# A gather-and-sum layer on one core: groups of 11 edge tiles made into batches of 22, each engine one batch behind its source, W1 applied after the last edge

## Chip, cores and metric

One core of a Trainium2 chip. The metric is the device time of one execution in microseconds (us); less is better.

## What is computed

A graph layer over 6,250 nodes of 96 features and 106,250 edges sorted by destination. Cut to what matters:

```python
h = jnp.maximum(_layernorm(x, axis=-1), 0.0)
ea = edge_attr @ W_edge.T + b_edge
msg = jax.nn.relu(h[src] + ea)
aggr = jax.ops.segment_sum(msg, dst, num_segments=N_NODES)
z = (1.0 + eps) * h + aggr
out = x + jax.nn.relu(z @ W1.T + b1) @ W2.T + b2
```

All data is float32. The edges make 830 tiles of 128 and a tail of 10.

## The kernel before

**Tiles and groups.** The 830 tiles are worked on in 77 groups (`group_sizes`, L43): 7 of ten tiles, 68 of eleven, 2 of six. In each group all but at most one tile get their rows `h[src]` by an indirect DMA that POOL issues (`gather`, L286: one instruction per tile). The eleventh tile is gathered by TensorE: a one-hot matrix (VectorE, `make_onehot`, L608, 125 x 6400 in bf16) times `h` split into three bf16 parts (`split_table`, L590), in 50 matmuls of 288 columns (`gather_by_matmul`, L390), which also add that tile's edge term (L396); VectorE then sums the three parts (L636).

**A group, by engine.** TensorE makes the edge terms of the ten tiles, two groups ahead (`edge_features`, L381, two banks per group, two groups of banks). VectorE adds the gathered rows, five tiles at once (L641). ScalarE applies relu (L362). TensorE multiplies each tile of messages by a 0/1 matrix `select` (VectorE, L546), which sums them by destination into a window of 128 nodes (L427). VectorE copies the window (L567), moves the offsets (L568), and makes the next `select`; TensorE multiplies the copy by W1 (L431); VectorE adds the product to `acc` (L578). A group has one window. `acc` so holds z @ W1 from the start.

**Order.** Each engine's program is written out by hand. TensorE per group g: sums of g, W1 of g (it waits for the copy), one-hot gather of g+1, edge terms of g+2 (L449 to L465). VectorE per group g: parts of g's one-hot gather (waits for TensorE), additions of g, one-hot of g+2, then the window of g (L619 to L662). POOL may be five groups ahead (`GATHER_RING`): it waits for VectorE's additions of g-5 (L306). SyncE loads edges three groups ahead, and the source numbers for the one-hots (`load_pe_src`, L249) in chunks of 17 tiles.

**Front.** Layernorm of all nodes in five chunks (VectorE statistics L510, ScalarE L333), the table `h` stored to DRAM (L247); POOL gathers 30 tiles of raw `x` meanwhile, which are normalised afterwards (L628 to L633, L355); table gathers wait for the store (L299). In groups 2 to 14 the term (1 + eps) * h @ W1 is made in 13 steps (transposes L440, copy L340, matmul L447, addition L586).

**End.** For ten blocks of 625 nodes: relu with b1 (L375), matmuls with W2 (L472), addition of x (L669), store (L272).

Of the kernel before, what the change touches and what calls it, by code (L numbers as in the profile page):

```python
# [7 lines left out]
ALU = mybir.AluOpType  # L8
# [7 lines left out]
GROUP_TILES = 10  # L16
# [4 lines left out]
RAW_GROUPS = 3  # L21
LAST_TILES = 6
PE_FROM = 7
PE_AHEAD = 2
SRC_CHUNK = 17
SPLITS = 3
GATHER_RING = 5
EDGE_RING = 3
NODE_PARTS = 125
NODE_RUN = 5  # L30
LN_COLS = 10
BASE_COLS = 4
BASE_FROM = 2
BOUND_ROWS = 80

# [7 lines left out]
def group_sizes(tiles):  # L43

    rest = tiles - 2 * LAST_TILES - PE_FROM * GROUP_TILES
    paired = rest // (GROUP_TILES + 1)
    assert paired * (GROUP_TILES + 1) == rest
    return [(GROUP_TILES, 0)] * PE_FROM + [(GROUP_TILES, 1)] * paired + [(LAST_TILES, 0)] * 2


def gnn_layer(nc, x, edge_t, src_tiles, pe_src, dst_tiles, dst_rows, w_edge_t, b_edge,
# [4 lines left out]
    pairs = group_sizes(TILES)  # L56
    sizes = [by_pool for by_pool, _ in pairs]
    tiles_of = [by_pool + by_pe for by_pool, by_pe in pairs]
    pe_index = [sum(by_pe for _, by_pe in pairs[:g]) if pairs[g][1] else None for g in range(len(pairs))]
    PE_TILES = sum(by_pe for _, by_pe in pairs)  # L60
    GROUPS = len(sizes)
    LAST = GROUPS - 1
    MOST = max(tiles_of)
    GE = MOST * EDGE_TILE
# [4 lines left out]
    HALF = HALF_TILES * D  # L69
    first_tile = [sum(tiles_of[:g]) for g in range(GROUPS)]  # L70
    halves = [[(t, min(t + HALF_TILES, n)) for t in range(0, n, HALF_TILES)] for n in sizes]
    adds_to = [sum(len(h) for h in halves[:g]) for g in range(GROUPS + 1)]
    gathers_to = [[sum(halves[k][i][1] - halves[k][i][0] for k in range(g % GATHER_RING, g + 1, GATHER_RING)
                       if i < len(halves[k])) for i in range(len(halves[g]))] for g in range(GROUPS)]
# [3 lines left out]
    SRC_CHUNKS = PE_TILES // SRC_CHUNK  # L78
    HS = SPLITS * D
    SRCS = SRC_CHUNK * EDGE_TILE  # L80
    assert sum(tiles_of) == TILES and PE_TILES % SRC_CHUNK == 0 and PE_FROM >= LN_CHUNKS + 1 and N == BLOCKS * BLOCK and COLS % LN_COLS == 0 and GROUPS <= BOUND_ROWS
    assert 0 < TAIL and HALF <= BANK and D + WINDOW // 4 == WINDOW and (RUN - 1) * D + WINDOW <= BANK
# [5 lines left out]
    with ExitStack() as ctx:  # L88
# [136 lines left out]
        def edges_of(g):  # L225
            return edge_t[:, first_tile[g] * EDGE_TILE:(first_tile[g] + tiles_of[g]) * EDGE_TILE]
# [49 lines left out]
        def _(pool):  # L276
# [18 lines left out]
            for g in range(RAW_GROUPS):  # L295
                for t in range(GROUP_TILES):
                    gather(x, g, t)
# [420 lines left out]
```

## Time and profile before

| | |
|---|---|
| median of 3 runs | 1468.35 us (1465.48 to 1468.41) |
| the profiled execution: time | 1468.4 us |
| its span, first to last instruction | 1466.3 us |
| mean granted TensorE clock | 0.858 of 2.4 GHz |
| POOL gathers of a tile | 762, and one of the tail |
| groups with a one-hot gather | 68 |

The time of the profiled execution is 2.1 us over its span. PE is TensorE's matmuls, PEld its weight loads, DVE VectorE, ACT ScalarE, POOL GpSimd, SPq SyncE's queue. A busy time counts neither register work nor waits, so an engine that is 56% busy can still set the time in a part of each period. L12 is line 12 of the kernel before. A timeline line has: start, duration, engine, line, operation, output<-input, count of merged instructions and, in brackets, the engine's idle time before it and what ended it.

### The profile page before, as it was taken

What the parts mean: (1) busy time and instruction counts of PE and PEld (TensorE: products, weight loads), DVE (VectorE), ACT (ScalarE), POOL (GpSimd) and SP (SyncE); (2) the same over time, 40 slices, a digit from 0 to 9 for tenths busy, and PEclk for the clock granted to TensorE, in tenths of its full rate; (3) what the DMA queues carried; (4) which work ended last, traced back from release to release, by engine and by line L of the source; (5) the groups of instructions that cost most, each with busy time, mean ns of one, the idle gap of its engine ahead of it and who ended that gap; (6) DMA issues with size and microseconds to landing.
All of it is one profiled execution on the core that took longest, in us unless ns stands there. A gap on an engine that the chain in (4) does not pass through costs nothing.

```text
span 1466.3 us, 18251 instructions
## 1 busy us (share of the span) xinstructions
PE 1033.7 (70%) x7058; PEld 842.1 (57%) x7058; DVE 825.7 (56%) x806; ACT 144.9 (10%) x270; POOL 731.9 (50%) x771
## 2 busy tenths in 40 slices
PE   2023477777677777777777777777777777777777
PEld 2023365555566666665666666665666666666566
DVE  4424556545555566656655656666566555656643
ACT  4302101001000001000000000000000000000002
POOL 7345654445455555555555555555555555555200
PEclk9966667988899989989889899999888899989985
DMA  8411131221422232222222322222222222222102
GB/s 217 103 40 39 44 94 47 51 54 42 113 64 60 57 86 70 61 59 60 58 60 60 87 58 60 70 59 60 58 60 56 60 60 57 65 64 60 37 9 66
DMA packets 39302, 94.84 MB, mean 65 GB/s; under 512 B 15049, under 2 KB 17549, under 8 KB 38719
## 3 DMA queue, kind: packets, MB, share of 16 engines
q1 hardware_dynamic: 14031, 55.61, 13.8%
q0 software_dynamic: 24416, 37.51, 12.6%
q8 instruction: 58, 0.95, 0.3%
q10 hardware_dynamic: 772, 0.57, 0.2%
q14 instruction: 25, 0.20, 0.0%
HBM read 88.82 MB, written 4.80 MB: 64 GB/s over the span
## 4 chain that ended last, share of the span: by engine, by line
PE 48%; DVE 26%; issue 19%; another core or an unknown queue 3%; ACT 3%; DVEq 2%
PE pe_ps L394 36%; DVE onehot L612 15%; DVE msg L641 6%; PE sums_ps L427 4%; PE sums_ps L431 3%; PE edge_ps L385 2%; PE edge_ps L472 2%; ACT msg L362 1%; DVE agg_sb L567 1%; PE pe_ps L396 1%; ACT gathered L355 1%; PE base_ps L447 1%; DVEq L622 1%; DVE stats L510 1%
## 5 line engine op out<-in xcount | busy, mean ns | idle before, releaser
L289 POOL DMA_INDIRECT gathered<-h_table,src_all x732 | 701.5, 958 | 616.8 <-DVE msg L641 415.0
L394 PE MATMUL pe_ps<-hs_or_hidden,onehot 125*128 125x288 bf16 x3400 | 538.6, 327 | 6.1 <-issue 4.3
L394 PEld LDWEIGHTS pe_ps<-hs_or_hidden,onehot 125*128 125x128 bf16 x3400 | 376.1, 112 | 156.4 <-issue 20.3
L612 DVE TENSOR_TENSOR onehot<-iota_bank,x_all 125x6400 bf16<-125x6400 f32 x68 | 463.4, 6815 | 0.1
L427 PE MATMUL sums_ps<-select,msg 128*96 128x128 f32 x1660 | 228.3, 301 | 136.5 <-ACT msg L362 123.5
L427 PEld LDWEIGHTS sums_ps<-select,msg 128*96 128x96 f32 x1660 | 213.2, 184 | 156.3 <-issue 156.3
L636 DVE TENSOR_REDUCE msg<-pe_ps 128x96 f32<-128x288 f32 x68 | 31.1, 458 | 396.0 <-PE pe_ps L396 393.1
L431 PE MATMUL sums_ps<-agg_sb,w 96*96 96x128 f32 x154 | 43.7, 374 | 233.8 <-DVE agg_sb L567 197.6
L385 PE MATMUL edge_ps<-w_edge,edge_in 97*128 97x96 f32 x1524 | 191.1, 283 | 22.4 <-DMA edge_in<-edge_t_dram 22.4
L362 ACT ACTIVATE msg<-msg 128x480 f32<-128x480 f32 (+2 forms) x154 | 94.5, 634 | 1106.0 <-DVE msg L641 1106.0
L385 PEld LDWEIGHTS edge_ps<-w_edge,edge_in 97*128 97x128 f32 x1524 | 184.6, 199 | 22.6 <-issue 22.6
L431 PEld LDWEIGHTS sums_ps<-agg_sb,w 96*96 96x96 f32 x154 | 23.0, 196 | 251.2 <-DVE agg_sb L567 211.3
L546 DVE TENSOR_TENSOR select<-iota_bank,dst_rel 128x1408 f32<-128x1408 f32 (+2 forms) x78 | 124.7, 1599 | 17.0 <-DVE dst_rel L568 12.8
L641 DVE TENSOR_TENSOR msg<-edge_ps,gathered 128x480 f32<-128x480 f32 (+1 forms) x154 | 92.6, 643 | 13.2 <-ACT gathered L355 11.3
L586 DVE TENSOR_TENSOR acc<-acc,base_ps 96x500 f32<-96x500 f32 (+1 forms) x13 | 13.6, 1048 | 96.8 <-PE base_ps L447 92.1
L567 DVE COPY agg_sb<-sums_ps 96x128 f32<-96x128 f32 x77 | 21.4, 278 | 52.9 <-PE sums_ps L427 21.6
L289 POOL DMA_INDIRECT gathered<-x_dram,src_all x30 | 28.5, 952 | 9.9 <-issue 8.8
L396 PE MATMUL pe_ps<-w_edge,edge_in 97*128 97x96 f32 x136 | 24.4, 260 | 0.0
L578 DVE TENSOR_TENSOR acc<-acc,sums_ps 96x128 f32 x77 | 21.1, 274 | 4.4 <-remote 4.4
L472 PE MATMUL edge_ps<-w,hs_or_hidden 97*125 97x128 f32 x100 | 22.1, 424 | 1.7 <-ACT hs_or_hidden L375 1.7
L472 PEld LDWEIGHTS edge_ps<-w,hs_or_hidden 97*125 97x125 f32 x100 | 21.8, 311 | 2.0 <-ACT hs_or_hidden L375 2.0
L396 PEld LDWEIGHTS pe_ps<-w_edge,edge_in 97*128 97x128 f32 x136 | 21.4, 191 | 1.7
(65 smaller groups left out, 179.1 us busy)
## 6 DMA issues: line engine op xcount, KB each, us to landing
edge_in<-edge_t_dram SPq DMA_DIRECT2D x68, 528.0 KB
gathered<-h_table,src_all POOLq DMA_INDIRECT x732
x_all<-pe_src_dram SPq DMA_DIRECT2D x4, 952.0 KB
edge_in<-edge_t_dram SPq DMA_DIRECT2D x7, 480.0 KB
x_all<-x_dram SPq DMA_DIRECT2D x5, 420.0 KB
h_table<-h_all SPq DMA_DIRECT2D x5, 420.0 KB
h_all<-x_dram SPq DMA_DIRECT2D x1, 2100.0 KB
out_dram<-h_all SPq DMA_DIRECT2D x10, 210.0 KB
```

Of the source, the lines that this page charges most:

```text
L289: nc.gpsimd.indirect_dma_start(out=gathered[slot][:, t * D:(t + 1) * D], out_offset=None, in_=table, in_offset=bass.IndirectOffsetOnAxis(a ...
L362: nc.scalar.activation(half, half, ACT.Relu).then_inc(relu_done, 1)
L385: mm = pe.matmul(edge_ps[g % 2][t // HALF_TILES][:, at:at + D], edge_in[g % EDGE_RING][:, t * EDGE_TILE:(t + 1) * EDGE_TILE], w_edge[:], s ...
L394: pe.matmul(pe_ps[:, 0:HS], onehot[k % 2][:, j, :], hs[:, j, :], start=(j == 0), stop=False)
L396: pe.matmul(pe_ps[:, 0:D], edge_in[g % EDGE_RING][:, sizes[g] * EDGE_TILE:tiles_of[g] * EDGE_TILE], w_edge[:], start=False, stop=True).the ...
L427: mm = pe.matmul(agg_ps[0:D, :], data, select[0:rows, t, :], start=(t == 0), stop=(t == tiles - 1))
L431: pe.matmul(z_ps[0:D, :], w1[:], agg_sb[:], start=True, stop=True).then_inc(fold_done, 1)
L472: mm = pe.matmul(edge_ps[c % 2][c // 2 % 2][0:NP, i * D:i * D + WINDOW], hidden_nodes[:, c, i, :], w2[:], start=True, stop=True)
L546: nc.vector.tensor_tensor(select[:, 0:tiles, :], iota_ps.unsqueeze(1).broadcast_to((128, tiles, WINDOW)), dst_rel[:, bass.ds(at, tiles)].u ...
L567: nc.vector.tensor_copy(agg_sb[:], agg_ps[0:D, :]).then_inc(agg_copied, 1)
L612: nc.vector.tensor_tensor(onehot[k % 2][:], column_ps.unsqueeze(2).broadcast_to((NP, COLS, EDGE_TILE)), node_of[:, at:at + EDGE_TILE].unsq ...
L641: nc.vector.tensor_tensor(msg[g % 2][:, t0 * D:t1 * D], edge_ps[g % 2][i][:, 0:(t1 - t0) * D], gathered[slot][:, t0 * D:t1 * D], ALU.add). ...
```

## The change

The tiles are worked on in 39 batches of two sides: 3 batches of 2 x 10 tiles, 34 of 2 x 11 (ten by POOL, one by TensorE on each side), one of 12 and one of 10. POOL's gathers (762 and the tail) and TensorE's one-hot gathers (68) stay the same in number. `GATHER_RING` 5 groups becomes `SLOTS` 2 batches, in gathers and in edges. Both sides share one `select` instruction and one set of edge banks; each side has its own window, so there are 39 rounds of sums for 77.

W1 is taken out of the windows (L431 and the copy L567 go; VectorE adds the sums straight to `acc`, once per side) and is applied after the last edge, per block of 625 nodes, in two matmuls of 320 and 305 columns (`hidden_sums`). The base term (1 + eps) * h is written to `acc` before the first window, by 13 groups of transposes and 13 VectorE instructions; it needs no matmul with W1. Only 20 tiles are gathered raw, 8 at once and 12 after the layernorm's second half. The layernorm's small operations are done for 20 and 30 columns instead of five times ten.

TensorE per turn c: sums of c-1, edge terms of c+1, one-hot gathers of c+1. VectorE per turn c: additions of c, parts of c's one-hot gathers, window of c-1, the two one-hots of c+2. Core of the diff:

```diff
-GROUP_TILES = 10
+SIDE_TILES = 10
+SIDES = 2
-GATHER_RING = 5
-EDGE_RING = 3
+SLOTS = 2
-SRC_CHUNK = 17
+SRC_CHUNK = 14
+PLAIN_BATCHES = 3
+LAST_SIDES = (6, 5)
+Z_SPLIT = 320
...
             # POOL
+            for s, t in first[:FIRST_BURST]:
+                gather(x, 0, s, t)
+            pool.wait_ge(norm_ready, 2)
+            for s, t in first[FIRST_BURST:]:
+                gather(x, 0, s, t)
             pool.wait_ge(src_rest_in, 16)
             pool.wait_ge(table_stored, 16 * len(spread) * LN_CHUNKS)
...
-            for g in range(RAW_GROUPS, GROUPS):
-                if g >= GATHER_RING:
-                    pool.wait_ge(added, adds_to[g - GATHER_RING + 1])
-                for t in range(sizes[g]):
-                    gather(h_table, g, t)
+            for c in range(1, BATCHES):
+                for s, t0, t1 in halves[c]:
+                    if c >= SLOTS:
+                        pool.wait_ge(added, adds_to[c - SLOTS] + half_at[c - SLOTS][(s, t0)] + 1)
+                    for t in range(t0, t1):
+                        gather(h_table, c, s, t)
...
             # TensorE
+            def edge_features(c):
+                pe.wait_ge(edges_in[c % SLOTS], 16 * (c // SLOTS + 1))
+                for i, (s, t0, t1) in enumerate(halves[c]):
+                    if c >= 1:
+                        before = half_at[c - 1][(s, t0)]
+                        pe.wait_ge(added, adds_to[c - 1] + before + 1)
...
+            def gather_by_matmul(c):
+                for s in range(SIDES):
+                    k = pe_before[c] + s
+                    pe.wait_ge(onehot_made, k + 1)
+                    if k >= SIDES:
+                        pe.wait_ge(pe_rows_summed, k - SIDES + 1)
...
-                    pe.wait_ge(agg_copied, this_window)
-                    pe.matmul(z_ps[0:D, :], w1[:], agg_sb[:], start=True, stop=True).then_inc(fold_done, 1)
...
+            for c in range(BATCHES):
+                if c >= 1:
+                    sum_windows(c - 1)
+                if c + 1 < BATCHES:
+                    if c == 0:
+                        pe.wait_ge(ones_set, 2)
+                    edge_features(c + 1)
+                    if has_pe[c + 1]:
+                        if pe_before[c + 1] == 0:
+                            pe.wait_ge(hs_made, LN_CHUNKS)
+                            pe.wait_ge(tail_added, 1)
+                        gather_by_matmul(c + 1)
+            sum_windows(LAST)
+
+            def hidden_sums(c):
+                if c >= 2:
+                    pe.wait_ge(mlp_relu_done, len(z_parts) * (c - 1))
+                for i, (n0, n1) in enumerate(z_parts):
+                    pe.matmul(z_banks[c % 2][i][0:D, 0:n1 - n0], w1[:], acc[:, c * BLOCK + n0:c * BLOCK + n1],
+                              start=True, stop=True).then_inc(z_done, 1)
...
             # VectorE
-                    nc.vector.tensor_copy(agg_sb[:], agg_ps[0:D, :]).then_inc(agg_copied, 1)
+                    dve.wait_ge(acc_summed, this_window)
+                    add_sums(0, firsts[0], done).then_inc(side_summed, 1)
...
                     make_select(dve.snap(over, min_val=at, max_val=at + step), widest)
-                    dve.wait_ge(fold_done, this_window)
-                    dve.wait_ge(acc_summed, this_window)
-                    nc.vector.tensor_tensor(acc[:, bass.ds(base, WINDOW)], acc[:, bass.ds(base, WINDOW)],
-                                            z_ps[0:D, :], ALU.add).then_inc(acc_summed, 1)
+                    dve.wait_ge(side_summed, this_window)
+                    add_sums(1, firsts[1], done).then_inc(acc_summed, 1)
...
+            for c in range(BATCHES):
+                slot = c % SLOTS
+                dve.wait_ge(edge_done, c + 1)
+                for s, t0, t1 in halves[c]:
+                    i = t0 // HALF_TILES
+                    dve.wait_ge(gather_in[slot][s][i], 16 * gathers_to[c][(s, t0)])
...
+                if has_pe[c]:
+                    for s in range(SIDES):
+                        at = s * side[c] + by_pool[c]
+                        dve.wait_ge(pe_gathered, pe_before[c] + s + 1)
...
+                if c >= 1:
+                    sum_windows(c - 1)
+                if c == 0:
+                    split_table([0, 1, 2])
+                if c == 1:
+                    split_table([3, 4])
+                if c + 2 < BATCHES and has_pe[c + 2]:
+                    if c == 2:
+                        dve.wait_ge(table_stored, 16 * len(spread) * LN_CHUNKS)
+                    make_onehots(c + 2)
```

## Rows read from the trace of the kernel before

**Rows 1.** The page: busy time by engine, and the chain that ended last, by engine.

```profile
PE 1033.7 (70%) x7058; PEld 842.1 (57%) x7058; DVE 825.7 (56%) x806; ACT 144.9 (10%) x270; POOL 731.9 (50%) x771
...
PE 48%; DVE 26%; issue 19%; another core or an unknown queue 3%; ACT 3%; DVEq 2%
```

**Rows 2.** The timeline of one group of eleven tiles, all engines but POOL.

```profile
705.95 2.40 PE L385 MATMUL edge_ps<-w_edge,edge_in 97*128 97x96 f32 x20
706.15 0.46 DVE L636 TENSOR_REDUCE msg<-pe_ps 128x96 f32<-128x288 f32 x1 [6.66 <-PE pe_ps L396]
...
706.53 1.21 DVE L641 TENSOR_TENSOR msg<-edge_ps,gathered 128x480 f32<-128x480 f32 x2
...
707.66 6.82 DVE L612 TENSOR_TENSOR onehot<-iota_bank,x_all 125x6400 bf16<-125x6400 f32 x1
...
708.77 2.62 PE L427 MATMUL sums_ps<-select,msg 128*96 128x128 f32 x22 [0.43 <-ACT msg L362]
...
714.39 0.28 DVE L567 COPY agg_sb<-sums_ps 96x128 f32<-96x128 f32 x1
...
714.72 0.46 PE L431 MATMUL sums_ps<-agg_sb,w 96*96 96x128 f32 x2 [3.33 <-DVE agg_sb L567]
...
714.96 1.62 DVE L546 TENSOR_TENSOR select<-iota_bank,dst_rel 128x1408 f32<-128x1408 f32 x1 [0.22 <-DVE dst_rel L568]
715.01 8.26 PE L394 MATMUL pe_ps<-hs_or_hidden,onehot 125*128 125x288 bf16 x50
...
723.51 0.46 DVE L636 TENSOR_REDUCE msg<-pe_ps 128x96 f32<-128x288 f32 x1 [6.73 <-PE pe_ps L396]
```

**Rows 3.** The timeline of PE: the last one-hot gather, and the end.

```profile
1408.21 6.29 PE L394 MATMUL pe_ps<-hs_or_hidden,onehot 125*128 125x288 bf16 x50
...
1414.53 1.50 PE L385 MATMUL edge_ps<-w_edge,edge_in 97*128 97x96 f32 x12
...
1440.87 22.05 PE L472 MATMUL edge_ps<-w,hs_or_hidden 97*125 97x128 f32 x100 [1.67 <-ACT hs_or_hidden L375]
```

**Rows 4.** Stretches by engine: busy PE, PEld, DVE, ACT, POOL, granted clock, DMA share, GB/s.

```profile
716.70:718.70 2.00, 2.00 (x10) 1.29 (x9) 0.08 (x1) 0.00 (x0) 1.62 (x2) 0.50 0.25 49
...
1410.20:1412.20 2.00, 2.00 (x19) 1.61 (x17) 0.00 (x0) 0.00 (x0) 0.00 (x0) 1.00 0.00 0
...
1450.00:1455.00 5.00, 5.00 (x25) 5.00 (x25) 1.91 (x3) 0.00 (x0) 0.00 (x0) 0.50 0.32 102
```

**Rows 5.** The timeline of POOL: one group's first gather; first and last of thirty; one slowed.

```profile
59.18 0.98 POOL L289 DMA_INDIRECT gathered<-h_table,src_all  x1 [0.30 <-issue]
...
95.47 0.95 POOL L289 DMA_INDIRECT gathered<-h_table,src_all  x1 [0.30 <-issue]
...
122.41 1.59 POOL L289 DMA_INDIRECT gathered<-h_table,src_all  x1 [0.30 <-issue]
...
708.01 0.95 POOL L289 DMA_INDIRECT gathered<-h_table,src_all  x1 [5.09 <-DVE msg L641]
```

**Rows 6.** The timeline of the front: ScalarE's layernorm, the first table gather, the first window.

```profile
30.53 3.69 ACT L333 ACTIVATE h_all<-x_all,shift,rstd 125x96 f32<-125x96 f32 x10 [10.96 <-DVE shift L504]
...
46.03 3.69 ACT L333 ACTIVATE h_all<-x_all,shift,rstd 125x96 f32<-125x96 f32 x10 [11.62 <-DVE shift L504]
...
57.99 0.89 POOL L300 DMA_INDIRECT tail_gathered<-h_table,src_all  x1 [17.73 <-DMA h_table<-h_all]
...
74.24 3.86 PE L427 MATMUL sums_ps<-select,msg 128*96 128x128 f32 x20 [12.97 <-issue]
94.29 0.29 DVE L567 COPY agg_sb<-sums_ps 96x128 f32<-96x128 f32 x1 [21.02 <-remote]
```

**Rows 7.** The timeline of DVE: two register reads between two instructions; the end.

```profile
179.52 1.08 DVE L586 TENSOR_TENSOR acc<-acc,base_ps 96x500 f32<-96x500 f32 x1 [0.88 <-remote]
180.91 1.22 DVE L641 TENSOR_TENSOR msg<-edge_ps,gathered 128x480 f32<-128x480 f32 x2 [0.30 <-issue]
...
1439.91 0.06 DVE L664 MEMSET eps_col<- 128x1 f32 x1
```

More of the change, by code:

```diff
@@ new lines, in _ @@
+            last.then_inc(raw_h_done, 1)
+            for c in range(BATCHES):
+                for i, (s, t0, t1) in enumerate(halves[c]):
+                    act.wait_ge(added, adds_to[c] + i + 1)
+                    end = t1
+                    if t1 == by_pool[c] and has_pe[c]:
+                        act.wait_ge(pe_rows_summed, pe_before[c] + s + 1)
+                        end = side[c]
+                    part = msg[c % 2][:, (s * side[c] + t0) * D:(s * side[c] + end) * D]
+                    nc.scalar.activation(part, part, ACT.Relu).then_inc(relu_done, 1)
+                if c == 1:
@@ L409, in _ @@
+            pe.wait_ge(base_put, BASES)
             pe.wait_ge(bounds_min_max, 2)
@@ L557, in _ @@
             over = dve.alloc_register("dve_over")
-            def sum_windows(g, first, last):
-                at = first_tile[g]
-                tiles = tiles_of[g] + (g == LAST)
-                step = 0 if g == LAST else tiles
-                widest = tiles if g == LAST else max(tiles, tiles_of[g + 1] + (g + 1 == LAST))
-                with dve.Fori(first, last + 1, WINDOW) as base:
+            below = dve.alloc_register("dve_below")
+            node = [dve.alloc_register(f"dve_node{s}") for s in range(SIDES)]
@@ new lines, in add_sums @@
+            def add_sums(s, first, at):
+                dve.reg_mov(node[s], first + at - N)
+                dve.reg_alu(below, node[s], 31, ALU.logical_shift_right)
+                dve.reg_mul(node[s], node[s], below)
+                dve.reg_add(node[s], node[s], N)
+                cols = bass.ds(dve.snap(node[s], min_val=0, max_val=N), WINDOW)
+                return nc.vector.tensor_tensor(acc[:, cols], acc[:, cols], agg_ps[0:D, s * WINDOW:(s + 1) * WINDOW],
+                                               ALU.add)
@@ new lines, in sum_windows @@
+            def sum_windows(c):
+                firsts = [dve.value_load(bounds_i[0:1, SIDES * c + s:SIDES * c + s + 1], min_val=0, max_val=N - 1)
+                          for s in range(SIDES)]
+                span = dve.value_load(bounds_i[0:1, 2 * BOUND_ROWS + c:2 * BOUND_ROWS + c + 1], min_val=0, max_val=N - 1)
+                at = first_tile[c]
+                tiles = tiles_of[c] + (c == LAST)
+                step = 0 if c == LAST else tiles
+                widest = tiles if c == LAST else max(tiles, tiles_of[c + 1] + (c + 1 == LAST))
+                with dve.Fori(0, span + 1, WINDOW) as done:
@@ L679 @@
     E, D = edge.shape
-    pairs = group_sizes(E // EDGE_TILE)
-    ends = np.cumsum([by_pool + by_pe for by_pool, by_pe in pairs])
-    pe_tiles = [end - 1 for end, (_, by_pe) in zip(ends, pairs) if by_pe]
+    plan = batch_plan(E // EDGE_TILE)
+    side_tiles = [n + p for n, p in plan for _ in range(SIDES)]
+    ends = np.cumsum(side_tiles)
+    pe_tiles = [end - 1 for end, p in zip(ends, [p for _, p in plan for _ in range(SIDES)]) if p]
     def by_tile(index):
```

596 lines of the change are left out of this document (285 added, 311 removed).

## The prediction

> **What bounds the kernel now.** Start with the page: no engine is busy over 70% of the span, and the chain that ended last is spread over TensorE, VectorE and "issue" [rows 1]. So look for a cycle, in the timeline of one group [rows 2]. Read it from one sum of one-hot parts (L636) to the next: 723.51 - 706.15 = 17.36 us. VectorE adds (to 707.66), makes the one-hot of 6.82 us, and only then reaches the copy of the window at 714.39, though TensorE had ended the sums at 711.39. TensorE waits 3.33 us for that copy, because W1 stands ahead of its gather. The gather's 8.26 us then keep VectorE idle for 6.73 us. Each engine so waits for the other once a group. POOL is no bound: it idles 5.09 us before a group's gathers [rows 5], waiting for additions.
>
> The gather of 8.26 us has a second cause. Its 2 us after 716.70 run at a granted clock of 0.50, that is 1.2 GHz, with 10 matmuls; after a wait of only 0.38 us the last gather takes 6.29 us at 1.00 (2.4 GHz), 19 matmuls in 2 us [rows 3, 4]. The long wait for the copy is what precedes the fall.
>
> **POOL's new period.** Thirty gathers in a row start at 59.18 to 95.47: 36.29 / 29 = 1.251 us each [rows 5], the unit of the sum. A batch has 20: **25.0 us**, against 2 x 17.36 = 34.7 now. It may start gathers of c once VectorE has added the same half of c-2, one whole batch earlier, so it should never wait once running.
>
> **TensorE per batch**, at full clock: two sums of 2.62 = 5.2; edge terms of 20 tiles, 2 x 2.40 = 4.8 [rows 2]; two gathers with their edge term, 1414.53 - 1408.21 = 6.32 each, 12.6 [rows 3]. In all 22.7. W1 (0.46) and its wait are gone. It has 2.3 us left under POOL's 25.0, and will spend them waiting for the last gathered half. A wait of 3.33 us came before a low clock, one of 0.38 didn't; 2.3 is between. A fall costs 8.26 - 6.29 = 2.0 us, which gives 24.7: still under 25.0. So I add nothing.
>
> **VectorE per batch**: additions 4 x 0.57 = 2.3 (707.66 - 706.53 is two), parts 2 x 0.38, offsets 0.2 with a wait of 0.2, two additions to `acc` at 0.28 (the copy is nearest), `select` 2 x 1.62 - 0.3 = 2.9, one-hots 2 x 6.8 = 13.6 [rows 2]. Sum 20.5. A register read costs about 0.7 us (1.39 between two instructions with two reads in between [rows 7]); three are exposed, 2.1, and I allow 0.7 for the arithmetic of the window addresses. 23.3, 1.7 under POOL. Its waits: additions of c+1 are queued behind the one-hots of c+2. Put the last addition of c at 0. Parts and reads end at 3, the window by 7, one-hots by 21, three additions by 23, and the last half lands at 25. The sums of c-1, for which the window waits, ended before 0. TensorE: quarter of the edge terms, gathers of c+1 to 14, sums of c to 19, three quarters of the next edge terms from 21 on (they wait for the additions) to 25. Nothing else is late; what is next is VectorE at 23.3.
>
> **ScalarE, SyncE.** Relus stay the same in number of columns and hide as now. Edge loads of a batch wait for the gather of c-2 and are needed over 25 us later; the row source chunks (now 14 tiles) are asked for seven batches ahead. Both cost nothing unless the period fell to 20.
>
> **The front.** The first table gather is at 57.99 [rows 6]. ScalarE idled 10.96 and 11.62 us there for VectorE's shifts, which no instruction shown explains; POOL's raw gathers and all the loads ran then. Now 8 raw gathers, not 22, run in that time. Bounds: 58 as before, 58 - 22.6 = 35. I take **42**, nearer the lower, since most gathers go. From here POOL's queue is the path, if VectorE is in time. POOL asks for the additions of batches 0 to 3 when it has issued the gathers of 1 to 4: 25, 50, 75 and 100 us after the store. VectorE's work from the layernorm's end to the additions of batch 3: base term 13 x 1.08 = 14 [rows 7]; the start of the windows 8 (a guess); norms of 20 raw tiles, which wait for 2 x 3.69 on ScalarE [rows 6], 7; four batches of additions 9; splits of h, 25 instructions of 960 columns at no more than 2 x 0.57, 28; three windows with their reads 18; two pairs of one-hots 27 [rows 2]. That is 111, of which 15 lie before the store's end (ScalarE's last three chunks, 11, and the store, 4): 96 against 100. Tight, so I put 5 us for waits of POOL; the ends are 0 and 21, the largest unexplained idle [rows 6].
>
> **POOL's stream.** 762 - 20 = 742 tiles and the tail: 743 x 1.251 = **930**. Some gathers take 1.59 us for 0.95 [rows 5], 0.64 more, while VectorE casts h or the node numbers: some 16 of them, **10**.
>
> **The end.** The last gather lands about 2 us on (between 0 and 4). Then additions and relu 1.2, VectorE's window of batch 37 (2 of work, 2.1 of reads), ten tiles and the tail on TensorE at half clock 2.85 + 0.4, the last window 2: **12** with the landing. It took 7.1 from the additions before. After it stood 1466.3 - 1439.91 = 26.4 us [rows 7], of which 22.05 are TensorE with W2, back to back, yet at 0.50 to the end [rows 3, 4]. W1 now joins on that path: a block has 625 columns against 5 x 128 = 640, at 22.05 / 640 x 625 = 21.5 for ten blocks. I take it at that price, as it is the nearest shape; at full clock both would be half. **48.**
>
> **Sum**: 42 + 5 + 930 + 10 + 12 + 48 = 1047 span, plus 2.1 outside it: 1049, and the profiled 1468.4 is the median of the runs to 0.1. Forecast **1050 us**. One per cent of slack in POOL's cadence is 9 us.
>
> On the end, the Trainium skill ("TensorE: Matmul & The Clock Gate", section "What's actually happening") says that sustained work lifts the clock. Here 22 us of it did not [rows 4]. By that rule the end would be about 20 us shorter and the sum 1030.
>
> **Rivals.**
> 1. *The end runs at full clock.* W1 streams 320 columns per weight load where W2 streams 128, and the clock may rise. Against: W2 alone stayed low. Saves (21.5 + 22) / 2 = 22, less some start: 1030. The page named above bears on this one. Chance 0.12.
> 2. *Another engine is the bound.* VectorE's 23.3 has unseen register work and waits; or TensorE's clock falls in the stretch of wait plus edge terms and stays low over the first gather: each further fall is 2.0. A period of 27 to 31 makes 34 x 2 to 34 x 6 more: 1120 to 1250, middle 1130. For: both slacks are under 2.5 us. Against: waits shrink as the engine becomes the bound. Chance 0.21.
> 3. *Slower: long runs of gathers hold the other engines.* In the run of thirty, TensorE's sums ended at 78.1 by their row, yet VectorE's copy that waits for them came at 94.29 [rows 6], 16 us later, about when the run ended at 96.4. In the steady part gathers pause 5.09 us each group, and no such hold is seen [rows 2, 5]. The change takes the pauses away. If every batch had one hold of 16: 25 + 16 = 41 per batch, 34 x 16 = 544 more, 1594. It decides from a hold of 12.3 us per batch (420 / 34). Against: other groups in the front overlapped gathers unharmed, so it looks bound to first use. Chance 0.03.
> 4. *POOL gains nothing*, because VectorE's additions come late each batch (the ring is 40 tiles, was 50): period as now, about 1468 + 22 - 60 of front; 1430. It takes 10 us more VectorE work than the rows hold. Chance 0.02.
>
> **Numbers.** Forecast 0.62. Range 1015 to 1140: downward a front of 35, no waits and half of rival 1's gain or more; upward a front of 58, waits of 21 and most of rival 2. A measurement here tells 0.2%, 3 us. Faster 0.96, same 0.01, slower 0.03: only rival 3 is slower.
>
> **What would show it.** Right: POOL over 85% busy-plus-issue from 45 to 980 us with starts 1.25 apart and no pause at a batch's edge; period 25.0; the longest idle of TensorE before edge terms, released by additions; granted clock over 0.95 in the steady part and 0.50 in the end; 43 us of matmuls at the end. Wrong: pauses of POOL released by additions (rival 2 or 4), a low clock during gathers, TensorE idle before its sums, or end signals that come long after their matmuls (rival 3).

## The result, and the profile after

The changed kernel takes **1622.0 us** (median of 4 runs, 1619.6 to 1629.4) where the kernel before takes 1468.4 beside it: a ratio of 1.105 (95% interval 1.101 to 1.110). It is slower by a tenth, and the forecast was 1050. The profiled execution is the one of 1622.13, its span 1620.3.

Later kernels were run in sets, each on one chip with the kernel before beside them, and the sets fell into two kinds. In some, the kernel before took 1448 to 1469 us as here, and in all of those TensorE was held in long runs of gathers: it issued far fewer instructions than it could, though the profile shows nothing that it waited for. In others the kernel before took 1396 to 1397, and no kernel was held. In one of the latter the changed kernel took **1027.1 us**. Both faces are needed to understand the numbers, so each time below says which it belongs to: "held" or "free".

The page after, held: busy time by engine, the chain by engine, and two groups (the last column is the idle time ahead of the group, and what ended most of it). Against [rows 1], TensorE's share fell and "issue" grew:

```profile
PE 1059.2 (65%) x6918; PEld 826.3 (51%) x6918; DVE 797.5 (49%) x614; ACT 131.1 (8%) x252; POOL 729.0 (45%) x771
...
PE 63%; issue 30%; DVE 3%; another core or an unknown queue 2%; ACT 1%; DVEq 0%; DMA 0%; SPq 0%
...
L295 POOL DMA_INDIRECT gathered<-h_table,src_all x742 | 708.0, 954 | 794.7 <-DVE msg L687 579.2
...
L404 PE MATMUL pe_ps<-hs_or_hidden,own_onehots 125*128 125x288 bf16 x1700 | 338.3, 338 | 263.9 <-issue 262.9
```

The last line is the odd one: 263.9 us in which TensorE stood ahead of a one-hot matmul with nothing to wait for. The other one-hot tile, same shape, has 3.2. The timeline of POOL after shows the rhythm; only gathers that do not follow their predecessor by 1.25 us are shown, and one that does:

```profile
643.77 0.95 POOL L295 DMA_INDIRECT gathered<-h_table,src_all  x1 [29.53 <-DVE msg L687]
...
673.27 0.94 POOL L295 DMA_INDIRECT gathered<-h_table,src_all  x1 [4.79 <-DVE msg L687]
...
727.34 0.95 POOL L295 DMA_INDIRECT gathered<-h_table,src_all  x1 [29.35 <-DVE msg L687]
728.60 0.95 POOL L295 DMA_INDIRECT gathered<-h_table,src_all  x1 [0.30 <-issue]
...
756.69 0.95 POOL L295 DMA_INDIRECT gathered<-h_table,src_all  x1 [4.65 <-DVE msg L687]
```

Two batches take 727.34 - 643.77 = 83.6 us, 41.8 each, not 25.0; POOL waits for additions, which wait for TensorE. The timeline of PE inside the run of gathers that begins at 727.34 tells what TensorE does:

```profile
740.23 0.41 PE L404 MATMUL pe_ps<-hs_or_hidden,own_onehots 125*128 125x288 bf16 x1 [0.20 <-issue]
741.67 0.40 PE L404 MATMUL pe_ps<-hs_or_hidden,own_onehots 125*128 125x288 bf16 x1 [1.03 <-issue]
743.07 0.40 PE L404 MATMUL pe_ps<-hs_or_hidden,own_onehots 125*128 125x288 bf16 x1 [1.00 <-issue]
...
754.33 1.10 PE L404 MATMUL pe_ps<-hs_or_hidden,own_onehots 125*128 125x288 bf16 x3 [1.00 <-issue]
755.73 4.98 PE L404 MATMUL pe_ps<-hs_or_hidden,own_onehots 125*128 125x288 bf16 x22 [0.30 <-issue]
```

One matmul in 1.40 us (740.23, 741.67, 743.07), though the profile shows nothing that it waits for, until 755.73: 3.7 us after the end of the twentieth gather (752.05). Then full speed. The windows after, with the columns of [rows 4], show a stretch between runs and one inside:

```profile
709.00:724.00 15.00, 15.00 (x127) 12.65 (x127) 14.97 (x5) 0.00 (x0) 0.00 (x0) 1.00 0.19 61
740.00:750.00 10.00, 3.07 (x9) 0.80 (x8) 7.22 (x2) 0.00 (x0) 7.56 (x9) 0.50 0.20 39
```

The same code, 127 matmuls in 15 us or 9 in 10. In every run of 20 between 600 and 900 us, TensorE first ran freely, for 7.2 to 7.5 us after the start of the first run of a pair and 10.1 to 10.8 us of the second; counted in the trace, that is 129 to 153 of its instructions (matmuls and weight loads together) each time.

The count is steadier when it takes in all engines. Take as the stop the first TensorE instruction that has at most nine in the 2.8 us from it on. Over the 29 unbroken runs of 20 past 200 us, TensorE then has issued 123 to 153 instructions (standard deviation 9.5), and all engines together 155 to 171 (4.2), whether the stop comes after 7 or after 11 us. In the first run of a pair VectorE has some 17 instructions in that time, in the second 3, and TensorE has the fewer or the more for it. So what runs out looks shared by the engines; TensorE, with most of the instructions, is the one that stands.

A hold is easy to count: matmuls with over 0.9 us of idle before them that ended in "issue". The changed kernel has 265 here, and none of the ten profiles of free sets has one.

### The profile page after: what moved, and what is told of

It reads as the page before. It is cut to its first block, busy times and chain, and to the rows that moved or that the text cites. A ratio compares the mean times of both kernels' runs of the same rounds, so it can differ in the third digit from the quotient of the medians.

```text
span 1620.3 us, 16935 instructions
## 1 busy us (share of the span) xinstructions
PE 1059.2 (65%) x6918; PEld 826.3 (51%) x6918; DVE 797.5 (49%) x614; ACT 131.1 (8%) x252; POOL 729.0 (45%) x771
## 3 DMA queue, kind: packets, MB, share of 16 engines
q1 hardware_dynamic: 9929, 55.73, 13.4%
## 4 chain that ended last, share of the span: by engine, by line
PE 63%; issue 30%; DVE 3%; another core or an unknown queue 2%; ACT 1%; DVEq 0%; DMA 0%; SPq 0%
PE pe_ps L404 34%; PE agg_ps L451 15%; PE edge_ps L392 10%; PE edge_ps L489 1%; PE pe_ps L407 1%; DVE acc L553 1%; ACT gathered L358 0%; ACT xh L344 0%; DMA xh<-x_dram 0%; PE pe_ps L477 0%; DVE msg L687 0%; DVE select L580 0%; DVEq L616 0%; PE agg_ps L477 0%
## 5 line engine op out<-in xcount | busy, mean ns | idle before, releaser
L404 PE MATMUL pe_ps<-hs_or_hidden,own_onehots 125*128 125x288 bf16 x1700 | 338.3, 338 | 263.9 <-issue 262.9
L404 PEld LDWEIGHTS pe_ps<-hs_or_hidden,own_onehots 125*128 125x128 bf16 x1700 | 181.1, 110 | 411.0 <-issue 357.4
L451 PE MATMUL agg_ps<-select,msg 128*96 128x128 f32 x1660 | 254.2, 313 | 107.2 <-issue 96.6
L451 PEld LDWEIGHTS agg_ps<-select,msg 128*96 128x96 f32 x1660 | 233.4, 194 | 134.9 <-issue 124.0
L673 DVE TENSOR_TENSOR own_onehots<-const_ps,xh 125x6400 bf16<-125x6400 f32 x34 | 230.3, 6813 | 0.1
L673 DVE TENSOR_TENSOR xh<-const_ps,xh 125x6400 bf16<-125x6400 f32 x34 | 230.3, 6813 | 0.1
L404 PE MATMUL pe_ps<-hs_or_hidden,xh 125*128 125x288 bf16 x1700 | 216.2, 287 | 3.2 <-issue 3.2
L369 ACT ACTIVATE msg<-msg 128x480 f32<-128x480 f32 (+1 forms) x154 | 91.5, 629 | 1394.7 <-DVE msg L687 869.2
L404 PEld LDWEIGHTS pe_ps<-hs_or_hidden,xh 125*128 125x128 bf16 x1700 | 167.0, 99 | 45.4 <-issue 4.6
L580 DVE TENSOR_TENSOR select<-const_ps,dst_rel 128x2816 f32<-128x2816 f32 (+3 forms) x40 | 120.1, 3002 | 5.8 <-issue 5.5
```

Source lines behind the costliest of these rows:

```text
L369: nc.scalar.activation(part, part, ACT.Relu).then_inc(relu_done, 1)
L404: pe.matmul(pe_ps[s][:, 0:HS], onehot[c % 2][s][:, j, :], hs[:, j, :], start=(j == 0), stop=False)
L451: mm = pe.matmul(agg_ps[0:D, s * WINDOW:(s + 1) * WINDOW], msg[c % 2][:, tile * D:(tile + 1) * D], select[:, tile, :], start=(t == 0), sto ...
L580: nc.vector.tensor_tensor(select[:, 0:tiles, :], iota_ps.unsqueeze(1).broadcast_to((128, tiles, WINDOW)), dst_rel[:, bass.ds(at, tiles)].u ...
L673: nc.vector.tensor_tensor(onehot[c % 2][s], column_ps.unsqueeze(2).broadcast_to((NP, COLS, EDGE_TILE)), node_of[:, at:at + EDGE_TILE].unsq ...
```

## The experiments

Theory S, from the trace: TensorE draws on a **stock of some 140 instructions' worth** of something that isn't refilled while gathers follow each other without a gap. Its rivals at first: another engine is late, or the length of the runs has nothing to do with it. Where no interval stands beside a time, it is of a single run.

**Leaving the gathers out.** The kernel `nogather` has none from batch 4 on; POOL writes scratch instead and VectorE adds stale rows.

```
-                    for t in range(t0, t1):
-                        gather(h_table, c, s, t)
...
+                    else:
+                        fill(t1 - t0)
```

> From batch 4 on the gathers are left out; POOL writes a scratch region instead, about as long as the gathers took (the messages are then made of old rows). Theory S (a run of gathers starves TensorE of instructions: some 130 to 150 of its instructions pass after a run's start, then one each 0.7 us until 3.6 us after its end): with no gathers nothing is held, a batch takes what the prediction's sum says, 23 to 28 us, and the time is 1050 to 1130 us. Rival W (the order of waits in the change, with its two slots, makes the pattern of 41 us): still near 1600 us.

Measured, free set: 922.1 us. The page:

```profile
PE 845.5 (92%) x6918; PEld 752.6 (82%) x6918; DVE 798.8 (87%) x614; ACT 129.4 (14%) x252; POOL 620.6 (67%) x909
...
PE 86%; DVE 7%; issue 2%; ACT 2%; DMA 1%; DVEq 1%; SPq 0%
```

TensorE is the bound at 21.9 us a batch (from its timeline in `storm`, below), so the forecast's 22.7 for TensorE was 0.8 high, and its 23.3 for VectorE at least 1.4 too high. No engine's own work makes 41 us.

**Pauses in POOL's stream**, first in the same free set. From batch 4 on, POOL fills scratch and waits for it: four fills ahead of each ten gathers (`pause10`, shown), or two ahead of each five (`pause5`).

```
+                        if c > PLAIN_BATCHES and issued % 10 == 0:
+                            fill(4)
                         gather(h_table, c, s, t)
+                        issued += 1
```

> The changed kernel, but POOL writes scratch for some 4 to 5 us ahead of each ten gathers. Theory S: runs of ten last 12.2 us, as in the kernel before, so TensorE is held little; a batch takes 2 x (12.5 + 4.5) = 34 us against 41.3, time 1370 to 1420 us. Rival M (each gather takes a fixed share of something that TensorE needs, however the gathers are grouped): no gain, 1620 or more.

> The same total of pauses, 2 to 2.5 us ahead of each five gathers. Theory S with a long recovery (the hold ended 3.6 us after a run's end): the pauses are too short to end a run, the hold stays, 1550 us or more. Theory S with a stock that refills in any gap: as with pauses ahead of each ten or better, 1370 to 1420 us. Rival M: 1620 or more in both.

Measured: 1249.8 and 1243.9 us, both POOL's stream with its pauses and nothing else: 25 + 6.2 us a batch. And the kernel before, with POOL's wait taken once for two groups so that its gathers come in runs of 20:

```
-                if g >= GATHER_RING:
-                    pool.wait_ge(added, adds_to[g - GATHER_RING + 1])
+                if g >= GATHER_RING and (g - GATHER_RING) % 2 == 0:
+                    pool.wait_ge(added, adds_to[min(g - GATHER_RING + 2, GROUPS)])
```

> The kernel before, but POOL waits once for two groups and then issues twenty gathers in a run. Theory S: TensorE is held in the second half of each run, for about 12 us per two groups less what was idle anyway (3.3 per group), 34 x 6 to 34 x 12 more: 1670 to 1880 us. Rival W and any theory that puts the cause into the rest of the change: 1468 us, as nothing else is changed.

Measured: 1397.8 us against 1396.5 for the kernel before, no hold at all. That would have refuted S, were it not that the kernel before itself took 1396.5 and not 1468, and that nothing was held in any of these four kernels, not even in `nogather`'s front. The set was free, and told nothing on S; the numbers that S had named for its four kernels were not tested there. So the main ones were run again.

> The changed kernel as it is, beside the kernel before on the same chip. In the last set the kernel before took 1396.5 us, not 1468.4, and a run of 73 gathers held TensorE for nothing. Theory S as first put (every long run holds TensorE): 1550 to 1620 us. Theory C (the hold is there in some places where a program runs and not in others; where it is absent nothing starves TensorE): a batch takes POOL's 25.0 us and the time is 1030 to 1090 us here, as in the prediction's sum, and the ratio to the kernel before is 0.74 to 0.78.

> Pauses of 1.6 us ahead of each five gathers. Where nothing is held the pauses only cost POOL's time: 31.3 us a batch, 1244 us, slower than the changed kernel by some 6.3 x 34 = 200 us. Where a long run holds TensorE: faster than the changed kernel by up to 370 us.

Measured, held (before 1467.5): 1626.3 us for the changed kernel (ratio 1.108, 1.106 to 1.111) and **1269.4 for the one with pauses** (ratio 0.865, 0.862 to 0.868). In its timelines, POOL and one batch of PE, the trickle is gone:

```profile
698.67 0.95 POOL L297 DMA_INDIRECT gathered<-h_table,src_all  x1 [0.27 <-POOL dst_all L319]
...
704.62 1.60 POOL L319 MEMSET dst_all<- 128x800 int32 x2
706.49 0.95 POOL L297 DMA_INDIRECT gathered<-h_table,src_all  x1 [0.27 <-POOL dst_all L319]
...
729.94 0.95 POOL L297 DMA_INDIRECT gathered<-h_table,src_all  x1 [0.27 <-POOL dst_all L319]
```

```profile
709.48 2.43 PE L406 MATMUL edge_ps<-w_edge,edge_in 97*128 97x96 f32 x10 [2.37 <-DVE msg L701]
714.65 2.45 PE L406 MATMUL edge_ps<-w_edge,edge_in 97*128 97x96 f32 x10 [2.73 <-DVE msg L701]
716.89 7.71 PE L418 MATMUL pe_ps<-hs_or_hidden,xh 125*128 125x288 bf16 x50
...
724.63 6.29 PE L418 MATMUL pe_ps<-hs_or_hidden,xh 125*128 125x288 bf16 x50
```

TensorE now waits for additions (2.37 and 2.73 us), because POOL, at 729.94 - 698.67 = 31.3 us a batch, is slower than it. The 1269.4 still has the held front, since the pauses begin with batch 4; free, the same kernel took 1243.9.

> The kernel before with POOL's runs of twenty, a second time: in the first set it took 1397.8 us beside 1396.5 of the kernel before, and nothing was held in that set. Where the kernel before takes 1467 us (holds are there): theory S says TensorE is held in each run of twenty, 1600 to 1880 us. Rival W: equal to the kernel before. Where the kernel before takes 1396 again, both say 1397 and nothing is told.

Measured, held (before 1459.3): **1852.1 us**. The kernel before, with nothing changed but its runs of gathers from ten to twenty, loses 393 us. Its timeline of PE in the run that begins at 739.06 and ends at 763.7:

```profile
751.84 2.49 PE L394 MATMUL pe_ps<-hs_or_hidden,onehot 125*128 125x288 bf16 x19
754.69 0.30 PE L394 MATMUL pe_ps<-hs_or_hidden,onehot 125*128 125x288 bf16 x1 [0.37 <-issue]
756.09 0.28 PE L394 MATMUL pe_ps<-hs_or_hidden,onehot 125*128 125x288 bf16 x1 [1.10 <-issue]
757.49 0.28 PE L394 MATMUL pe_ps<-hs_or_hidden,onehot 125*128 125x288 bf16 x1 [1.12 <-issue]
...
767.31 4.16 PE L385 MATMUL edge_ps<-w_edge,edge_in 97*128 97x96 f32 x19 [0.38 <-issue]
```

The same signature in other code: 141 instructions from the start of the run, then the trickle, then 3.6 us past the last gather. Since TensorE had waits of its own in this run, the stop came only after 15 us: a count, not a time. Over its 31 runs of 20 past 200 us, by the rule above, the stop comes after 127 to 149 instructions of TensorE as in the changed kernel, but at 11.7 to 15.4 us in place of 6.9 to 11.1. (So a slow refill with time does not explain the changed kernel's 125 at 7 us and 143 at 10.7 either: at 13.6 us it would give 157, and the mean here is 135.) This is the run that shows the cause, since nothing but the length of the runs was changed; it also ends the rival that the rest of the change is at fault.

**How long must a pause be, and how often?**

> Pauses of 3.2 us ahead of each ten gathers, in the place where holds are: runs of ten last 12.2 us. Theory S with a stock of 130 to 145 instructions: TensorE runs through that in 7 to 10 us, so each run of ten holds it for some 2 to 5 us, 1270 to 1450 us; with pauses ahead of each five it took 1269.

> One scratch write of about 0.4 us ahead of each five gathers, in place of two of 0.8. If the pause's time is what refills TensorE's instructions, a quarter of it is too little: holds are back in part, 1300 to 1500 us where holds are. If any break in the run is enough: POOL's 20 x 1.25 + 4 x 0.4 = 26.6 us a batch, 1269 - 34 x 4.7 = 1110 us.

> The same with a scratch write of one column, about 0.1 us. If any break is enough: 25.5 us a batch, 1075 us. If the time of the pause counts: near the changed kernel, 1500 to 1626 us where holds are.

Measured, held (same set): 1345.0, 1712.5 and 1617.8 us. With 3.26 us ahead of each ten, 57 of 63 runs of ten still reach the stop near their end (after 129 to 155 instructions, in many until 2 us after the run), so POOL waits. With 0.12 us ahead of each five it is the changed kernel again. With 0.45 us it is worse than no pause, which I had not expected: POOL's gathers then join into runs of 40, and TensorE is held through two batches (why they join isn't shown). Ahead of each five, a pause of 0.45 us buys nothing, and one of 1.6 us all that can be had.

How late TensorE recovers grows with the run: about 2.1 us after the last of ten, 3.3 to 3.9 after twenty, 6.6 after forty (`half_pe_c`, below). That is 0.15 us for each gather on top of about 0.6, as if something needed 1.25 + 0.15 = 1.40 us for a gather and fell behind. As an estimate from these, 5 x 0.15 = 0.75 us ahead of each five would let it catch up, between the pause that failed and the one that sufficed; and forty gathers with eight pauses of 0.45 should recover after 0.6 + 40 x 0.15 - 8 x 0.42 = 3.2 us. `short5` recovered after 4.0 to 4.1 in its runs of forty, so the estimate is 0.8 short.

**A count or a time; a shorter pause; the front.** `few_pe` leaves out half of each one-hot sum:

```
-                    for j in range(COLS):
+                    for j in range(0, COLS, 2):
```

and `half_pe` keeps the 50 matmuls but leaves out half of their columns:

```
-                        pe.matmul(pe_ps[s][:, 0:HS], onehot[c % 2][s][:, j, :], hs[:, j, :],
+                        width = HS if j == 0 else HS // 2
+                        pe.matmul(pe_ps[s][:, 0:width], onehot[c % 2][s][:, j, :], hs[:, j, 0:width],
```

> The kernel after, with the matmuls of a one-hot gather made over every second column alone: 25 of 288 columns for each tile in place of 50 (the other half of the sum is left out). TensorE's work in a batch falls from 22.7 to about 16.4 us and its instructions from about 380 to about 280; the runs of 20 gathers stay. Theory S (a stock of 120 to 150 instructions is used up in the run, and is not refilled while gathers follow each other): TensorE stops after the same 120 to 150 instructions of each run, and after the run 280 - 140 - 28 = some 110 instructions are left, 6.5 us: 28.7 + 6.5 = about 35 us for a batch in place of 41.3, about 1435 us. Theory T (TensorE is cut off a fixed 7 to 11 us after the run begins, whatever it has issued): 28.7 + 16.4 - 9 - 1.5 = 34.6 us for a batch, about 1425 us. The two differ in the run beside it, where the count stays and the time falls. If the runs of gathers hold nothing here, about 1140 us.

> The kernel after, with the matmuls of a one-hot gather all 50 in number, but over 144 of their 288 columns (the first alone over all; the rest of the sum is left out). TensorE's work in a batch falls to about 16.6 us as in the run beside it, but its instructions stay at about 380. Theory S: it stops after the same 120 to 150 instructions, which it now reaches earlier, some 5 to 8 us into a run, and some 210 are left after the run, about 9.5 us: about 38 us for a batch, about 1525 us. Theory T: it stops 7 to 11 us into the run as before, so after more instructions (170 to 220), and a batch takes 34.6 us as in the run beside it, about 1425 us.

> The kernel after with one pause of some 1.2 us (a memset of 1200 columns, waited for) ahead of each five gathers, from batch 4 on. With 1.6 us the holds were gone, with 0.45 us they were not. If 1.2 us are enough, POOL sets the time: 25.0 + 4 x 1.3 = some 30.2 us for a batch in place of 31.2, about 1240 us. If not, a batch goes on taking 41 us or more, 1600 to 1700 us; between the two if some of the pauses take and some do not.

> The kernel after with 1.6 us of pause ahead of each five gathers from batch 1 on, not from batch 4 on. Theory S: the holds of the front (TensorE trickling from 139 to 176 us) go too: three batches of 41 us become three of 31, 1269 - 30 = about 1240 us. If the front's slowness is its own (the base term behind the reads of the run of 33), the pauses cost 3 x 6.2 us there: about 1285 us. Where runs of gathers hold nothing, about 1260 us.

Measured, in a free set (before 1395.9): 1028.1, 1027.8, 1174.8 and 1260.6 us (the last with ratio 0.903, 0.901 to 0.904). Free, they settle neither count against time, nor the shortest pause, nor the front. They show two other things. Halving TensorE's one-hot work changes nothing: POOL's gathers are the whole time. And pauses cost what they last: 1.12 us ahead of each five is 148 us over 1027.

> The kernel after, unchanged, beside a kernel before that takes either about 1396 or about 1467 us. Where it takes 1396, runs of gathers hold TensorE in no kernel: the stream of 743 gathers then sets the time as in the forecast, 25.1 us a batch, and the kernel after takes some 1030 to 1055 us. Where it takes 1467, about 1622 us again.

> The kernel half_pe again (50 matmuls for each tile over 144 columns in place of 288). Where the kernel before takes about 1467 us: theory S (a stock of instructions) 120 to 150 instructions before TensorE stops, 5 to 8 us into a run, some 38 us for a batch, about 1525 us; theory T (a fixed time) 170 to 220 instructions before it stops at 7 to 11 us, 34.6 us for a batch, about 1425 us. Where the kernel before takes 1396: 1028 us again, POOL's stream alone.

Measured, free again (before 1396.9): 1027.7 for the second, and **1027.1 us for the changed kernel, ratio 0.736 (0.733 to 0.738)**. Its page, and its timeline of POOL (the gather of the tail, the first of the table and the last of all):

```profile
PE 900.3 (88%) x6918; PEld 786.5 (77%) x6918; DVE 795.8 (78%) x614; ACT 129.4 (13%) x252; POOL 729.4 (71%) x771
...
POOL 63%; issue 22%; DVE 6%; PE 4%; DMA 3%; ACT 1%; DVEq 1%; SPq 0%; POOLq 0%
```

```profile
37.87 0.88 POOL L309 DMA_INDIRECT tail_gathered<-h_table,src_all  x1 [0.30 <-issue]
39.05 0.97 POOL L295 DMA_INDIRECT gathered<-h_table,src_all  x1 [0.30 <-issue]
...
972.42 0.95 POOL L295 DMA_INDIRECT gathered<-h_table,src_all  x1 [0.30 <-issue]
```

POOL issues 755 gathers from 22.89 to 973.37 without one pause. This is the profile that the forecast described: the same instructions, in a run 755 long, and TensorE busy through it, as the window of 400 us shows:

```profile
460.00:860.00 400.00, 377.26 (x3004) 328.52 (x3002) 327.23 (x194) 37.65 (x64) 302.83 (x319) 0.94 0.38 86
```

**What is it that backs up?** Two runs, in a held set again (before 1447.8). In `storm` POOL makes, from batch 4 on, 12 small writes, each raising a semaphore, in place of each gather.

```
+                for i in range(times * TINY_WRITES):
+                    nc.gpsimd.memset(dst_all[:, i:i + 1], 0).then_inc(fill_step, 1)
+                fills[0] += times * TINY_WRITES
+                pool.wait_ge(fill_step, fills[0])
```

> The kernel after without its gathers from batch 4 on (the sums use stale rows), and in place of each gather 12 writes of one column by POOL, each of which raises a semaphore: some 10 instructions and 10 semaphore events in a microsecond, without a transfer. Theory R (what holds TensorE is the stream of recorded events, which a run of gathers fills with its 16 landings each, and which backs up into TensorE where its records are drained slowly): where the kernel before takes about 1467 us, TensorE is held here too, at one instruction in some 0.7 us within POOL's bursts, and a batch takes clearly more than POOL's own 25 to 30 us. Theory G (the gathers' transfers or descriptors hold TensorE): it is held nowhere, and the time is POOL's or TensorE's alone, 950 to 1150 us. Where the kernel before takes 1396 us, the second under both.

> half_pe a third time (50 matmuls for each tile over 144 columns in place of 288). Where the kernel before takes about 1467 us: theories S and R (a stock that each instruction uses up) 120 to 150 instructions before TensorE stops, 5 to 8 us into a run, some 38 us for a batch, about 1525 us; theory T (a fixed time) 170 to 220 instructions before it stops at 7 to 11 us, 34.6 us for a batch, about 1425 us. Where the kernel before takes 1396: 1028 us.

Measured: 958.3 and 1647.4 us. In `storm` TensorE isn't held anywhere past the front (timelines of POOL and of PE):

```profile
709.90 2.04 POOL L320 MEMSET dst_all<- 128x1 int32 x60 [12.85 <-DVE msg L707]
```

```profile
708.39 4.97 PE L468 MATMUL agg_ps<-select,msg 128*96 128x128 f32 x44
...
730.28 4.97 PE L468 MATMUL agg_ps<-select,msg 128*96 128x128 f32 x44
```

Theory R falls in the form it was given: 240 instructions and 240 semaphore events within 9 us (four bursts of 60) do not hold TensorE, which keeps 730.28 - 708.39 = 21.9 us a batch. The writes were faster than I had reckoned (0.034 us each), so a burst is shorter than a run of gathers; a longer one wasn't tried, and neither were the landing events of a gather's transfers. Of what was tried, only gathers hold TensorE. `storm` is also what `nogather` could not be, a kernel without gathers in a held set: its front is held, its steady part isn't.

`half_pe_c` halves TensorE's one-hot work at the same number of instructions, and takes 25 us *more* than the changed kernel did in its first, held set. Inside a run of gathers, windows and timeline of PE:

```profile
734.10:747.50 13.40, 13.29 (x77) 0.50 0.18 38
760.00:790.00 30.00, 4.16 (x14) 0.50 0.15 33
```

```profile
783.33 0.28 PE L405 MATMUL pe_ps<-hs_or_hidden,own_onehots 125*128 125x144 bf16 x1 [2.52 <-issue]
786.13 0.28 PE L405 MATMUL pe_ps<-hs_or_hidden,own_onehots 125*128 125x144 bf16 x1 [2.52 <-issue]
787.53 0.28 PE L405 MATMUL pe_ps<-hs_or_hidden,own_onehots 125*128 125x144 bf16 x1 [1.12 <-issue]
788.24 0.29 PE L405 MATMUL pe_ps<-hs_or_hidden,own_onehots 125*128 125x144 bf16 x1 [0.43 <-issue]
```

TensorE stopped after 154 and 157 instructions, 12 to 13 us into the run; over all 13 runs of forty it was 147 to 159. T had said 170 to 220 at 7 to 11 us and falls. S had said 120 to 150 at 5 to 8 us: its count is nearly met, its time is not, since the first matmuls of a run went at a granted clock of 0.50 (77 in 13.4 us). Its 38 us a batch was wrong too (42.7), because POOL's runs joined to forty, as in `short5`. Late in such a run a matmul comes every 2.80 us, twice the 1.40 of a gather above, and after its last gather (ends at 783.8) in the end every 0.70.

**What stays open** is what the stock consists of. Against a lack of fetched instructions speaks the view of DMA queues of the changed kernel, held, for 739 to 742 us:

```profile
q8 instruction: 1, 0.02, 1.9%
```

A block of 16 KB landed at 739.74, in 0.94 us, well inside a hold. This queue moved 55 such blocks in the whole run, one for each 252 of TensorE's 13,836 matmuls and weight loads, so they are taken here for TensorE's instructions; in the 5 us behind it TensorE issued 11 instructions. Such blocks took 1.15 us on average in the held profile and 1.13 in the free one. Nor do the gathers' own transfers differ: their packets took 45 ns at the median held, 52 free. What does differ is how their landings are recorded: the trace of the changed kernel has 3,695 landing events held and 13,590 free, for the same 763 gathers, so the page has no time to landing where gathers hold, and has one where they do not (the changed kernel held, and `pause5` free):

```profile
gathered<-h_table,src_all POOLq DMA_INDIRECT x742
```

```profile
gathered<-h_table,src_all POOLq DMA_INDIRECT x742, 2.5
```

So in held sets a path that reports landings seems crowded, and if instructions need it too, a stock that all engines share is what one would see. This is argued, not shown. The Trainium skill ("NOTIFIC — the notification-queue block", section "7.1 Overflow: three behaviours, one of which stalls the engine") says that the block that writes trace records always holds its producers back rather than lose one inside. By that rule the hold may belong to being profiled; the fewer landing events and the shared count would agree, `storm` speaks against it for POOL's events, and no run here is of a kernel that isn't recorded. Nor is it shown what makes a set held or free: two chips had both.

## Why the prediction was wrong

**The step that failed** is one sentence in rival 3, "it looks bound to first use". With it the hold got a chance of 0.03, and the sum has nothing for it. The forecast had found the idle stretch in the front of the kernel before (16 us, from 78.1 to 94.29, in the run of thirty [rows 6]) and had named the right cause: the change takes the pauses of 5.09 us away [rows 5]. The runs showed a hold in every run of twenty.

**The price of that rival came right by luck.** It put one hold of 16 us on top of POOL's 25.0, which gives 41 a batch and 1594 us; measured were 41.8 and 1622. But TensorE is held from some 8.9 us after a run's start (the mean of the 29) to 24.7 + 3.7 = 28.4 us, so for 19.5 us a batch, and what that comes on top of is its own work of 21.9. As an estimate from these, 41.4: another hold on another engine's time, with nearly the same sum.

**What spoke against it** was that "other groups in the front overlapped gathers unharmed" and that the steady part shows no hold. The steady part could not speak against a hold at twenty: its runs have ten gathers, and from 400 us on TensorE issues at most 112 instructions in one, fewer than the 123 at which it was first seen to stop. POOL's pauses had been called "no bound"; in a held set they are what keeps TensorE supplied. `before_runs20_b` shows it with the kernel before.

The front was rightly taken for a sign, but the count does not explain it. `before_runs20` has the same front and was free, and its copy comes as soon as the sums end (52.66 + 4.55 = 57.21):

```profile
52.66 4.55 PE L427 MATMUL sums_ps<-select,msg 128*96 128x128 f32 x20 [12.91 <-ACT msg L362]
57.24 0.29 DVE L567 COPY agg_sb<-sums_ps 96x128 f32<-96x128 f32 x1 [5.56 <-PE sums_ps L427]
```

ScalarE's idle 10.96 and 11.62 us, which "no instruction shown explains" (rows 6), are missing there too, and its first gather of the table is at 40.59 in place of 57.99. So these waits belong to the held kind of set. But at 78.1 TensorE had issued only 59 instructions since the run began (129 with all engines), and in the run of twenty that begins at 134.98 it issued 215 without a hold, where some gathers came 1.6 to 1.9 us apart. Why is open; the count of some 140 is read from the steady parts alone.

**The rest of the sum** can be read on the free run, where no hold covers it: 1025.8 span against 1047.

- *Front to the first table gather*: 42 forecast, 37.9 measured.
- *Waits of POOL*: 5 forecast, 1.5 for all additions together.
- *POOL's stream*: 930 + 10 forecast; 973.4 - 37.9 = 935.5 measured, 1.259 for each of 743. It is the bound throughout, as forecast.
- *From the last gather to the MLP*: 12 forecast, 988.74 - 973.37 = 15.4 measured. Missed was a memset of 5.27 us that stands on VectorE ahead of the last additions.
- *The MLP*: 48 forecast, 37.1 measured, in both sets. Rival 1 came true by half. Its timeline in the changed kernel, held (MLP from 1583.31), and its window:

```profile
1583.31 0.06 DVE L718 MEMSET eps_col<- 128x1 f32 x1
```

```profile
1590.84 2.21 PE L489 MATMUL edge_ps<-w,hs_or_hidden 97*125 97x128 f32 x10
1592.89 0.70 PE L477 MATMUL pe_ps<-acc,w 96*96 96x320 f32 x2
1593.43 0.68 PE L477 MATMUL const_ps<-acc,w 96*96 96x305 f32 x2
1593.94 2.21 PE L489 MATMUL edge_ps<-w,hs_or_hidden 97*125 97x128 f32 x10
```

```profile
1610.00:1615.00 5.00, 5.00 (x24) 4.69 (x24) 0.81 (x2) 1.23 (x3) 0.00 (x0) 1.00 0.31 96
```

The granted clock is 1.00 (2.4 GHz), where [rows 4] had 0.50. W1 takes 1593.94 - 1592.89 = 1.05 us a block, half of the 2.15 reckoned (its first two blocks, still at 0.50, took 1587.69 - 1583.42 = 4.27, which is that price); but ten matmuls with W2 take 2.21, as the 22.05 for a hundred at half clock [rows 3]. The faster clock is worth 11 us, not 22. The Trainium skill's rule ("TensorE: Matmul & The Clock Gate", section "What's actually happening") that sustained work lifts the clock agrees with this end, at 1.00, and not with that of the kernel before, at 0.50 through 22.05 us of matmuls [rows 3, 4].

Of the signs named ahead: the one for rival 3, "TensorE idle before its sums, or end signals that come long after", is what the held profile showed, as "issue"; POOL's pauses released by additions, named there for rivals 2 and 4, came with it. VectorE's select (3.09) and one-hots (13.54 for two) came at their prices of 2.9 and 13.6.

## What to carry to other kernels

A hold seen once in a profile, with its mechanism and its price worked out, is not disposed of by a steady part that never enters its condition: ask which run length and which overlap the change creates, and whether any part of the profile has them. Where TensorE stands at "issue" while gathers stream, look at the length of the runs and the gaps between them before looking at any wait. And a price that comes out right does not show that its terms are. Time the kernel before beside each experiment: only its 1396 against 1468 told that a set of runs could say nothing on the theory.

The version with 1.6 us of pause ahead of each five gathers beats the kernel before in both kinds of set (1269 against 1467, 1244 against 1396, the latter of one run). The changed kernel as it is, is the best of all where gathers hold nothing, 1027, and the worse of the two where they do.

## What the runs showed of the hardware that was not expected

- In held sets, gathers issued one in 1.25 us stop TensorE, in the steady part, after 123 to 159 of its instructions, matmuls and weight loads alike, at whatever time that falls (6.8 to 15.4 us into the run); it then issues a matmul each 0.70, 1.40 or 2.80 us, and is free again 2 to 7 us after the run's end.
- In the changed kernel the stop is steadier in instructions of all engines (155 to 171) than in TensorE's own (123 to 153). In the other kernels the mean of all engines is 162 to 185, so this too is no constant.
- The same program on the same kind of chip is held or not held as a whole: 1622 or 1027 us. The kernel before, with short runs, differs by 5% only.
- Held, a pause of 0.45 us ahead of each five gathers made things worse (1712 against 1622), and one of 1.6 us cured them (1269).
- W2's matmuls (97 rows, 128 columns, f32, each with a weight load) take 0.22 us at either level of the clock (22.05 for a hundred at 0.50, 2.21 for ten at 1.00); W1's of 305 to 320 columns halve.
